# Rows by time then channel, 128-row score operands and a changed turn of the engines in a two-layer metaformer

## The reference

```python
def _attention(x, W1, W2, requires_value):
    sh = x.shape
    xf = x.reshape(sh[0], sh[1], -1)
    left = xf @ W1 @ W2
    att = softmax(einsum('bnd,bmd->bnm', left, xf) / sqrt(xf.shape[-1]))
    return (att @ xf).reshape(sh) if requires_value else att

def conv_ref(x, ...):                       # both layers
    x_res = conv2d(swapaxes(x, 1, 2), res_w, res_b)
    xc = swapaxes(_attention(swapaxes(x, 1, 2), W1_c, W2_c, True), 1, 2)   # 16 x 16 over channels
    xt = swapaxes(_attention(swapaxes(xc, 1, 3), W1_t, W2_t, True), 1, 3)  # 12 x 12 over times
    s = _attention(xt, W1_s, W2_s, False)                                  # 512 x 512 over nodes
    h = einsum('bnm,bmct->bnct', s * A[None], xt)
    g = einsum('bnct,cf->bnft', h, W_gcn)
    y = relu(conv2d(swapaxes(g, 1, 2), tcn_w, tcn_b, pad_t=1) + x_res)
    z = transpose(y, (0, 3, 2, 1))
    z = (z - mean(z)) / sqrt(var(z) + 1e-05) * ln_g + ln_b                 # over 16 channels
    return transpose(z, (0, 2, 3, 1))

x = x + conv_ref(_ln_c(x), ...)
t = _to_tokens(x)                           # 192 tokens of 512 features an item
t = t + _L0_ffn_ref(_ln_t(t), ...)          # mixture of 8 experts, top 2, with a capacity
x = _from_tokens(t, x)
x = x + conv_ref(_ln_c(x), ...)
t = _to_tokens(x)
t = t + _L1_ffn_ref(_ln_t(t), ...)          # 8-bit activations, ternary weights, squared ReLU
x = _from_tokens(t, x)
```

## Time and profile before

| | us |
|---|---|
| median of 3 runs | 2010.32 (2008.23 to 2010.35) |
| profiled execution | 2011.67 |
| its span | 2009.8 |
| graph convolution, layer 0 (from 184.0 to 534.6) | 350.6 |
| graph convolution, layer 1 (from 1365.0 to 1715.5) | 350.5 |
| experts (from 700 to 1125) | 425 |
| feed-forward of layer 1 (from 1760) | 248 |

### The profile page before, as it was taken

One profiled execution on the slowest core, in us unless ns is written; L12 is line 12 of the kernel. 1 busy time (PEld: TensorE's weight loads), 2 busy tenths in 40 slices (PEclk: granted clock), 3 DMA queues, 4 the chain that ended last, 5 costly groups with the idle time before them and its releaser, 6 DMA issues. The chain is left out here.

```text
span 2009.8 us, 28802 instructions
## 1 busy us (share of the span) xinstructions
PE 1512.1 (75%) x8454; PEld 1195.0 (59%) x8454; DVE 1219.3 (61%) x2496; ACT 716.8 (36%) x1149; POOL 484.2 (24%) x854
## 2 busy tenths in 40 slices
PE   4588999999364299999999433497999997057776
PEld 3466777777242278888888323295777775045554
DVE  4621678787466654444444277413787877578986
ACT  3312344444143033333332122122444443067765
POOL 1100134344310411111110256000344435002111
PEclk8678999999698589999999755697999999578988
DMA  6432021212175134344441677243112121013231
GB/s 185 133 86 64 24 64 55 63 55 63 55 226 172 30 98 122 117 121 121 121 122 40 191 233 238 72 117 108 56 55 70 55 63 48 24 48 93 72 94 55
DMA packets 152117, 192.30 MB, mean 96 GB/s; under 512 B 11801, under 2 KB 103417, under 8 KB 152061
## 3 DMA queue, kind: packets, MB, share of 16 engines
q1 hardware_dynamic: 101165, 116.47, 19.9%
q10 hardware_dynamic: 41680, 46.82, 7.5%
q0 software_dynamic: 9216, 28.32, 4.7%
HBM read 125.51 MB, written 66.06 MB: 95 GB/s over the span
## 5 line engine op out<-in xcount | busy, mean ns | idle before, releaser
L914 ACT ACTIVATE L_e<-g_s,L_nm 128x512 f32<-128x512 f32 x128 | 88.0, 687 | 287.2 <-DVE L_nm L750 286.4
L706 PE MATMUL g_y<-L_z,L_pt 128*128 128x192 f32 x1024 | 187.8, 326 | 0.5 <-ACT L_pt L922 0.5
L706 PEld LDWEIGHTS g_y<-L_z,L_pt 128*128 128x128 f32 x1024 | 169.9, 189 | 1.7 <-ACT L_pt L922 1.7
L1198 POOL DMA_INDIRECT x_xin<-xn_rows,x_index x64 | 66.1, 1033 | 295.6 <-PE ex_t L1212 147.2
L870 POOL TENSOR_TENSOR L_xr<-L_xr,L_lnb 128x192 f32<-128x192 f32 x128 | 84.3, 687 | 217.4 <-DMA L_xr<-x 115.4
L877 POOL TENSOR_TENSOR L_t<-L_rstd 128x48 f32<-128x48 f32 x96 | 35.6, 371 | 321.2 <-DVE L_rstd L811 316.2
L673 PE MATMUL g_z<-L_kw,L_xnT 96*128 96x192 f32 x512 | 97.0, 344 | 15.4 <-DVE L_v L780 15.4
L1292 DVE TENSOR_TENSOR x_mid<-ex_g,x_sig 128x480 f32<-128x480 f32 (+1 forms) x48 | 31.4, 654 | 122.7 <-ACT x_sig L1367 122.7
L673 PEld LDWEIGHTS g_z<-L_kw,L_xnT 96*128 96x128 f32 x512 | 87.1, 198 | 27.7 <-DVE L_v L780 27.7
L759 DVE SCALAR_TENSOR_TENSOR L_p<-L_e,L_rl,L_adj 128x512 f32<-128x512 f32 x128 | 96.7, 756 | 4.7 <-DVE L_rl L757 0.3
L750 DVE TENSOR_REDUCE L_nm<-g_s 128x1 f32<-128x512 f32 x128 | 87.9, 687 | 13.7 <-PE g_s L682 8.3
(11 more groups left out here) (273 smaller groups left out, 3885.8 us busy)
## 6 DMA issues: line engine op xcount, KB each, us to landing
xn_rows<-L_xnT SPq DMA_DIRECT2D x48, 384.0 KB, 3.8
L_xnT<-xn_rows SPq DMA_DIRECT2D x48, 384.0 KB, 3.4
y_slots<-x_yo ACTq DMA_DIRECT2D x64, 240.0 KB
x<-L_y ACTq DMA_DIRECT2D x32, 384.0 KB, 3.3
L_xa<-in_x SPq DMA_DIRECT2D x16, 384.0 KB, 4.1
L_raw<-xn_rows SPq DMA_DIRECT2D x16, 384.0 KB, 3.5
L_xr<-in_x SPq DMA_DIRECT2D x16, 384.0 KB, 3.4
L_xa<-x SPq DMA_DIRECT2D x16, 384.0 KB, 4.1
```

Source lines behind the costliest of these rows:

```text
L706: last = nc.tensor.matmul(out, pt[k % 2][:, P * c:P * c + P], z[q][:, c, :], start=False, stop=(c == NK - 1))
L914: nc.scalar.activation(e[k % 2][:, :], pss[k % 2][:, :], ACT.Exp, bias=s.nm2[:, k % 2:k % 2 + 1], accum_out=s.l[:, k % 2:k % 2 + 1]).then_ ...
L1198: nc.gpsimd.indirect_dma_start(xin[t % 4][:, :], None, tokens, bass.IndirectOffsetOnAxis(ap=index[q][:, t:t + 1], axis=0)).then_inc(x_in[t ...
```

## The change

- The 192 rows and columns of an item are in the order of time then channel everywhere: in the input as the host lays it out, in `wm`, `res`, the masks and the fold matrices. A half of 96 rows now holds six times of all channels. The mean and variance over channels read contiguous elements. `rc` and `rct` are the same for both halves and have one copy, `rt` has two. The channel attention reads contiguous columns. `res` is block-diagonal by half, and each half multiplies its own 96 columns; the bias row is in both.
- u and v are 128 partitions high, the rows from 30 on are set to zero once, by four memsets at the start of the stage. The projections have 96 rows out.
- ScalarE copies z. VectorE takes the maximum of row tile 2 before the centring, and the residual sum after row tile 3.
- SP stores the slab and loads xnT three items ahead in its program text, at the same point of the turn.
- `route` counts places over both halves of an item, since the experts' order of tokens stays that of channel then time. The last sum of `feed_forward` reads in the order of time then channel and writes to a buffer `yo` in the order of the reference, in steps of 12 elements.

```diff
 def small_attention(nc, s, tag, chan):
-    xa = s.shared[:, 0:B * NK * CT].rearrange("p (b k c t) -> p b k c t", b=B, k=NK, c=C)
+    xa = s.shared[:, 0:B * NK * CT].rearrange("p (b k x w) -> p b k x w", b=B, k=NK, w=W)
...
-                        rhs = xa[:, :, k, :, x] if chan else xa[:, :, k, x, :]
-                        last = nc.tensor.matmul(psp[PROJ * k:PROJ * k + PROJ, 0:n_all], w[:, k, x, :], rhs,
+                        last = nc.tensor.matmul(psp[PROJ * k:PROJ * k + PROJ, 0:n_all], w[:, k, x, :],
+                                                xa[:, :, k, x, :],
...
 def graph_conv(nc, s, tag, xn_rows, x_in, x_out, prefetch=None):
-        oct_ = lambda t: t[:, :, :].rearrange("p k (o t) -> p k o t", t=T)
-        lanes = lambda t: t.unsqueeze(2).to_broadcast([P, NK, O, T])
-        gain = lambda t: t[:, :].rearrange("p (o x) -> p o x", x=1).to_broadcast([P, O, T])
+        oct_ = lambda t: t[:, :, :].rearrange("p k (t o) -> p (k t) o", o=O)
+        flat = lambda t: t[:, :, :].rearrange("p k t -> p (k t)")
+        lanes = lambda t: flat(t).unsqueeze(2).to_broadcast([P, NK * T, O])
+        gain = lambda t: t[:, :].unsqueeze(1).to_broadcast([P, T, O])
...
+                def store(b, q):
+                    sp.wait_ge(out_done, ready(b))
+                    sp.dma_start(x_out[b], y[q][:, :, :]).then_inc(sent[q], 16)
+
                 load(0, 0)
                 if prefetch:
                     prefetch(sp)
-                with sp.Fori(0, B // 2 - 1) as i:
+                load(1, 1)
+                for q in range(2):
+                    load_residual(q, q)
+                load(2, 0)
+                with sp.Fori(0, B // 2 - 2) as i:
                     for q in range(2):
-                        load(i * 2 + q + 1, 1 - q)
-                        load_residual(i * 2 + q, q)
+                        load(i * 2 + q + 3, 1 - q)
+                        store(i * 2 + q, q)
+                        load_residual(i * 2 + q + 2, q)
...
-                        last = nc.tensor.matmul(psz[0:NPROJ, 1, :], kw[q][0:HALF, h, 0:NPROJ], xnT[q][0:HALF, h, :],
+                        last = nc.tensor.matmul(psz[0:HALF, 1, :], kw[q][0:HALF, h, 0:HALF], xnT[q][0:HALF, h, :],
...
-                    nc.tensor.matmul(pss[k % 2][:, :], u[q][0:KR, P * k:P * k + P], v[q][0:KR, :],
+                    nc.tensor.matmul(pss[k % 2][:, :], u[q][:, P * k:P * k + P], v[q][:, :],
...
-                    nc.tensor.matmul(out, xnT[q][0:HALF + 1, 0, P * k:P * k + P], s.res[0:HALF + 1, 0, :],
-                                     start=True, stop=False)
-                    nc.tensor.matmul(out, xnT[q][0:HALF, 1, P * k:P * k + P], s.res[0:HALF, 1, :],
-                                     start=False, stop=False)
+                    for h in range(2):
+                        nc.tensor.matmul(out[:, HALF * h:HALF * h + HALF], xnT[q][0:HALF + 1, h, P * k:P * k + P],
+                                         s.res[0:HALF + 1, h, :], start=(h == 0), stop=False)
...
+                for padded in (*u, *v):
+                    nc.vector.memset(padded[:, :].bitcast(F32), 0.0)
...
-                    step(nc.vector.tensor_reduce(s.mu[:, :, :], y[q][:, :, :].rearrange("p k (o t) -> p k t o", t=T),
-                                                 AX, ALU.add))
+                    step(nc.vector.tensor_reduce(flat(s.mu), oct_(y[q]), AX, ALU.add))
...
 def feed_forward(...):
-                        nc.gpsimd.tensor_tensor(ya[q][:, :, :], ya[q][:, :, :], xr[q][:, :, :],
-                                                ALU.add).then_inc(out_done, 1)
+                        in_time = lambda t: t[:, :, :].rearrange("p k (t c) -> p k t c", c=C)
+                        pool.wait_ge(sent[q], dma_free(i))
+                        nc.gpsimd.tensor_tensor(yo[q][:, :, :].rearrange("p k (c t) -> p k t c", t=T),
+                                                in_time(ya[q]), in_time(xr[q]), ALU.add).then_inc(out_done, 1)
```

More of the change, by code:

```diff
@@ L432, in small_attention @@
         part = s.z0[:, :, :].rearrange("p k x -> p (k x)")[:, 0:n_all]
[L433 to L434 removed]
+        fold = (lambda h: s.foldc[:, :]) if chan else (lambda h: s.foldt[0:n_half, h, :])
+        halves = range(1) if chan else range(2)
         with nc.Block() as block:
@@ L462, in _ @@
                         pe.wait_ge(turned_sb, g + 1)
-                        for h in halves:
-                            last = nc.tensor.matmul(psf[g][0:HALF, 256 + n_half * h:256 + n_half * h + n_half],
-                                                    fold(h), s.spt[0:n_half, g, 0:n_half], start=True, stop=True)
+                        last = nc.tensor.matmul(psf[g][0:HALF, 256:256 + n_half], fold(0),
+                                                s.spt[0:n_half, g, 0:n_half], start=True, stop=True)
                     last.then_inc(folded, 1)
@@ L964, in _ @@
                 item_turns(act, turn)
-                for q in range(2):
-                    act.wait_ge(sent[q], dma_ready(B // 2 - 1))
 def expert_weights(sp, s, d, e):
```

192 lines of the change are left out of this document (104 added, 88 removed).

## The result

The changed kernel takes 1922.4 us in the median against 2010.3 for the kernel before on the same chip: a ratio of 0.956, 95% interval 0.954 to 0.958. Three of its four launches took 1922.0 to 1922.5 us; the fourth took 1980.5 at a lower granted clock (0.79 for 0.85), and the ratio leaves it out. The profiled execution took 1922.03 us with a span of 1920.2. The forecast was 1912 us in a range of 1892 to 1948: the direction and the range were right, the saving was 88 us for 98, and its largest term, the scores, holds only beside the earlier row maximum.

What follows compares the result with a forecast made beforehand. TensorE's own work, with two waits, was taken to set the graph convolution's turn. Saving 3.06 us a turn (19.81 to 16.75) and other terms gave 49.0 a layer, 98 for two: 2010.3 - 98 = 1912 us, range 1892 to 1948.

Steps and rivals of the forecast that it cites:

- Scores: Graph convolution, score matmuls padded from 30 to 128 rows: 0.38 us saved at three scores, 0.28 at one, 1.42 a turn.
- Row maximum first: Graph convolution, VectorE's maximum of row tile 2 ahead of the centring: TensorE's wait at the projections goes, 0.98 us a turn.
- Residual matmuls: Graph convolution, block-diagonal residual with records 0.09 us apart: 0.29 saved a spread, 0.87 a turn over three spreads.
- The new wait: Graph convolution, the last spread waits for the transposed probabilities of its own tile: 0.21 us a turn added.
- Projections and the fourth spread: Graph convolution: their gains go into the slab convolution wait, growing from 0.35 to about 0.8 us; both counted at nothing.
- The rest of a layer: Graph convolution beyond 13 turns: 4.2 us first two turns, 0.4 fill, 1.7 last turn, 1.1 tail reductions, less 2.0 memsets.
- The channel attention: Its projections read contiguous columns: 3.0 us saved at full clock, some 0.8 in fold matmuls and copies, per layer.
- Copy of z: Graph convolution, copy moved from VectorE to ScalarE: VectorE falls from 15.8 to about 13.8 us a turn, off the path.
- Feed-forward: GpSimd's sum writes with a step of 48 bytes: counted at 0, bound 17 us over 16 items.
- That VectorE's idle time stays: Rival 1, graph convolution: VectorE's 3.98 us idle a turn remains, turn 17.8, 28 us more, 1940 us; chance 0.17.
- That the padding does nothing: Rival 2, score matmuls: padding to 128 rows saves nothing, 44 us missing, 1956 us; chance 0.10.
- The slower side, by the scattered write: Rival 3, feed-forward: GpSimd's scattered write decides from 6.1 us more an item; at 8.5 the time is 2019; chance 0.02.

Runs made afterwards that it cites:

- the run with 30 rows: The changed kernel with the score matmuls back at 30 rows instead of 128, buffers still 128 high and cleared: 1958.5 us, ratio 0.974.

## Why the prediction was nearly right

**Bound.** TensorE sets the turn: shown. Its 95.6% with one wait at the slab convolution is what the views of before promised.

**Scores, 1.42 a turn.** The mechanism is shown by the run with 30 rows, the size was 1.44, of which 1.21 is to be had in the changed kernel. But the prediction let the term stand by itself, and it doesn't: in the order of before it is worth nothing in a turn without a fall of the clock, and -1.0 in the mean. Its sign, a matmul 0.23 behind a score, didn't come: it is 0.32, between the 0.23 and the 0.42 of the rival.

**Row maximum first, 0.98 a turn.** The wait was gone, and alone it is worth 1.05. As a part of the change it is worth 85 us. The prediction took the wait's size before as the edit's value; what it missed is that every other saving ahead of the projections, scores and residuals, would have made that wait longer, and that the longer wait brings the clock down. The sum came out because both were in it, which is luck as far as the prediction's reasons go.

**Residual matmuls, 0.87 a turn: mis-sized.** 0.24 a spread in the records and 0.03 lost behind them, 0.21 for the 0.29 expected, 0.63 in three spreads. The step that failed is the spacing of 0.09, taken from transposes for plain matmuls; it is 0.105 in the mean of four records. This is 0.24 x 26, 6 us of the 10 that are missing.

**The new wait, 0.21.** 0.19 between residual and spread (0.61 for 0.42), and 0.07 in the spread itself.

**Projections and the fourth spread, counted at nothing.** The wait at the slab convolution grew by 0.35 (0.8 forecast, 0.70 measured), so the fourth spread is absorbed; the projections are not wholly, back at 62 rows they cost 0.14.

**A turn:** 19.82 - 1.44 - 1.05 - 0.63 + 0.26 + 0.03 = 16.99 by these, 16.96 in the trace, 16.75 forecast. The 1.05 is the score to the projections, 1.48 less the 0.43 of the run with 30 rows; the 0.03 is the wait's 0.39 more less 0.36 that the projections, the transposes and the fourth residual lose.

**The rest of a layer.** Predicted 47.2 for the graph convolution, 43.6 and 42.0 measured: 13 turns give 36.9 for 39.8 (the term above), the first two 5.1 and 3.3 for 4.2, the fill nothing for 0.4, the last turn with the tail 1.6 and 1.8 for 2.8. That tail isn't TensorE's. VectorE there:

```profile
471.97 0.95 DVE L809 TENSOR_REDUCE L_mu<-L_y 128x48 f32<-128x768 f32 x1
472.95 0.36 DVE L810 TENSOR_SCALAR L_mu<-L_mu 128x48 f32<-128x48 f32 x1
...
475.17 1.28 DVE L837 TENSOR_TENSOR L_y<-L_d,L_xr 128x768 f32<-128x768 f32 x1 [0.54 <-POOL L_d L899]
```

The reduction gains its 0.55, and then VectorE waits 0.54 for GpSimd's gains. The step that failed is the 1.1 of the two reductions in the tail: from the last but one division (L830) to the end of the last residual sum (L837) VectorE takes 15.8 us where it took 15.4.

The channel attention gave 5.1 and 5.6 for 3.8. Its projections take 6.66 us in layer 0, from the first record to the last, where they took 10.30:

```profile
101.10:104.50 3.40, 3.40 (x33) 1.78 (x37) 0.00 (x0) 0.00 (x0) 0.00 (x0) 0.50 0.02 5
104.50:107.76 3.26, 3.26 (x67) 2.01 (x60) 0.00 (x0) 0.00 (x0) 0.00 (x0) 1.00 0.00 0
```

Sixteen records take 0.86 for 1.79 at the clock of 1.00, and 1.68 to 1.71 for 1.77 to 1.79 at 0.50: at the low clock the contiguous columns gain nearly nothing, as the prediction had it. The projections gave 3.6 for the 3.0 because the clock also rose 0.8 us sooner after their start (3.4 for 4.2), which no run ties to the change, and the rest of the stage gave 1.4 and 1.8 for 0.8. In the other traces with the change the stage gains 4.4 to 6.4. The memsets cost 2.3 for 2.0.

**Copy of z, counted at nothing:** worth 0.3 a turn, 8 to 9 us, as the run with it on VectorE shows. The undone edit shows a wait for ScalarE's copies, so VectorE's fall from 15.8 to 13.8 was not all off TensorE's path: the 16.96 holds a 0.3 that no term of the sum gives.

**Route, counted at nothing:** 2.6 longer in this trace, 1.1 to 2.2 in the others that have it, against the "under 1 us either way" of the prediction. The prefix sums are sixteen records for four at a clock near the lower level:

```profile
L1062 PE MATMUL rt_pre<-r_hot,r_tri 96*96 96x128 f32 x16 | 4.0, 434 | 28.7 <-DVE r_hot L1101 28.7
```

**Feed-forward, 0 with a bound of 17:** 1.5 longer, of which the write can hold 16 x 0.02 = 0.3; in the other traces of the stage with the change it takes 252.2 to 255.5 us, so the 1.5 isn't told from none. The estimate of 0.9 us an item from the Trainium skill's read side ("GPSIMD Engine Reference", performance pitfalls) doesn't carry over to a write: no part of it is there.

**Rivals.** That VectorE's idle time stays (17.8 a turn) fell: 16.96. That the padding does nothing fell by the run with 30 rows. The slower side, by the scattered write, fell by its 1.83 us. The mechanism that could have ended there wasn't among them: an edit that speeds TensorE up to a wait that another engine fixes, here the padding without the order, ends 1.7% slower.

**Open.** The second normalisation runs the same code and took 2.3 longer here; in the other traces of the changed kernel it is 0.6 to 2.6 longer. No run was made for it.

## What to carry to other kernels

Before summing savings on the bounding engine, mark the waits that other engines fix: what is saved ahead of such a wait goes into it until the releasing chain is moved, so the move and the savings have to be valued together, once with and once without. Then look at the length to which a wait may grow: waits of 1 us cost only themselves here, most of those of 2.1 us took the clock of the work behind them too. And place a wait at the first instruction that needs it (the second half of the slab convolution, u without v): two such lines and a reordered clearing were worth 33 to 36 us (by the ratios and by the medians).
